# A recurrent mixer begins at step 15 + 7m instead of with pass m, inside a pipelined mixture of experts

## The reference

```python
xn = layernorm(x)
# the mixer, per sequence
xx = shift(xn) - xn
r, alpha, g = sigmoid((xn + xx*x_c) @ W_c.T)      # c = r, a, g
decay = exp(-softplus((xn + xx*x_w) @ W_w.T))
k = tanh((xn + xx*x_k) @ W_k.T);  v = (xn + xx*x_v) @ W_v.T
state_t = state_{t-1} * decay_t + alpha_t * k_t * v_t    # along the 256 tokens
m = r * state;  mn = groupnorm(m, groups of 8 channels) * gn_w + gn_b
s = (mn * g) @ W_out.T + b_out
# the experts, on all 4096 tokens: 4 rounds over the same 4 experts
cur = xn
for rnd in range(4):
    top2 of cur @ Wg[rnd] + bg[rnd]; cw = their softmax weights
    cur = cur + sum_e cw_e * (gelu(cur @ W1[e] + b1[e]) @ W2[e] + b2[e])
out = x + s * silu(cur)
```

## The kernel before

| stage | VectorE, ahead of `g_low_part` | TensorE, behind `down(s)` | ScalarE, ahead of `hidden` |
|---|---|---|---|
| 0 | `mixer_input` job 0 (L620 to L632) | `project` r, w: 6 matmuls | |
| 1 | `mixer_input` job 1 | `project` a, g | `take_rw` |
| 2 | `mixer_input` job 2 | `project` k, v | `take_ag` |
| 3 | `mixer_scan` (L638 to L644) | `turn_mixer`: 2 transposes | `take_kv` |
| 4 | `mixer_norm` (L651 to L660, 17 instructions) | | |
| 5 | | `turn_mixer`: 2 transposes | |
| 6 | `mixer_gate` (L667 to L674) | `W_out`: 3 matmuls (waits for `go_ready`) | |
| 7 | | | `take_s`: writes `s` over `xn_t[:, m]` |

## Time and profile before

### The profile page before, as it was taken

How to read it: one execution, slowest core, us unless ns; L and a number is a source line. 1 busy time by engine, 2 the same in 40 slices (tenths; PEclk the granted TensorE clock), 3 DMA queues, 4 the chain that set the end, 5 groups by cost and what they waited for, 6 DMA issues and landing times.

```text
span 860.7 us, 10675 instructions
## 1 busy us (share of the span) xinstructions
PE 806.1 (94%) x3640; PEld 648.5 (75%) x3640; DVE 748.0 (87%) x1442; ACT 641.4 (75%) x882; POOL 150.4 (17%) x167
## 2 busy tenths in 40 slices
PE   3788999899999999999999999999999999999994
PEld 3566777677778888788878888788878888788883
DVE  7799999999989888887988978897988879898884
ACT  3466767677768887878778887788878888688872
POOL 6022241331111111111111111011111111111111
PEclk7799999999999999999999999999999999999997
DMA  7123442343335342443325332344315433263534
GB/s 218 50 34 90 86 86 39 85 87 95 77 57 134 93 99 37 114 100 70 86 37 148 92 94 38 87 99 98 95 29 146 118 95 60 60 165 95 132 66 85
DMA packets 40581, 76.94 MB, mean 89 GB/s; under 512 B 6480, under 2 KB 18896, under 8 KB 36432
## 3 DMA queue, kind: packets, MB, share of 16 engines
q0 software_dynamic: 18432, 33.56, 23.0%
q1 hardware_dynamic: 21808, 42.69, 15.6%
q10 hardware_dynamic: 288, 0.02, 0.0%
HBM read 40.34 MB, written 2.36 MB: 50 GB/s over the span
## 4 chain that ended last, share of the span: by engine, by line
PE 66%; DVE 25%; ACT 5%; issue 3%; DMA 1%; SPq 0%; DVEq 0%; ACTq 0%; POOLq 0%
PE h_bank L767 10%; PE h_bank L766 10%; PE h_bank L765 10%; PE y_bank L811 10%; PE y_bank L807 10%; PE y_bank L806 10%; DVE g_lo L566 6%; ACT g L377 3%; DVE tmp L577 2%; ACT g_hi L381 2%; PE p_bank L765 2%; PE p_bank L767 1%; PE p_bank L766 1%; DVE xm L624 1%; DVE lgt L526 1%
## 5 line engine op out<-in xcount | busy, mean ns | idle before, releaser
L377 ACT ACTIVATE g<-h_bank,b_c 128x512 f32<-128x512 f32 x512 | 329.8, 681 | 98.7 <-PE h_bank L767 97.5
L566 DVE TENSOR_TENSOR g_lo<-g,g_hi 128x1024 fp32r<-128x1024 f32 x256 | 309.0, 1224 | 72.5 <-ACT g_hi L381 70.9
L381 ACT ACTIVATE g_hi<-g 128x1024 fp32r<-128x1024 f32 x256 | 271.7, 1061 | 8.1
L346 POOL DMA_DIRECT2D cur<-tmp x128 | 114.0, 891 | 693.6 <-DVE tmp L577 558.7
L765 PE MATMUL h_bank<-cur_lo,w_hi 128*128 128x512 f32 x512 | 207.5, 405 | 0.0
L767 PE MATMUL h_bank<-cur_hi,w_hi 128*128 128x512 f32 x512 | 204.8, 400 | 0.0
L766 PE MATMUL h_bank<-cur_hi,w_lo 128*128 128x512 f32 x512 | 204.2, 399 | 0.0
L806 PE MATMUL y_bank<-g_hi,w_hi 128*128 128x512 f32 x512 | 202.5, 396 | 0.0
L807 PE MATMUL y_bank<-g_hi,w_lo 128*128 128x512 f32 x512 | 202.2, 395 | 0.0
L811 PE MATMUL y_bank<-g_lo,w_hi 128*128 128x512 f32 x512 | 141.0, 396 | 0.5 <-DVE g_lo L566 0.4
L767 PEld LDWEIGHTS h_bank<-cur_hi,w_hi 128*128 128x128 f32 x512 | 97.3, 190 | 23.6
(11 more groups left out here) (115 smaller groups left out, 581.2 us busy)
## 6 DMA issues: line engine op xcount, KB each, us to landing
cw_b<-cw_scratch SPq DMA_DIRECT2D x32, 1024.0 KB, 5.7
cur<-tmp POOLq DMA_DIRECT2D x128, 256.0 KB, 3.4
cur<-in_x SPq DMA_DIRECT2D x8, 256.0 KB, 4.8
xr<-in_x SPq DMA_DIRECT2D x8, 256.0 KB, 5.5
out<-o SPq DMA_DIRECT2D x8, 256.0 KB, 3.5
g<-in_w SPq DMA_DIRECT2D x4, 256.0 KB, 5.5
cw_scratch<-cw SPq DMA_DIRECT2D x32, 8.0 KB, 1.4
cw_b<-in_proj_t SPq DMA_DIRECT2D x1, 384.0 KB, 3.3
```

Of the source, the lines that this page charges most:

```text
L346: pool.dma_start(cur[:, s // E % NB * BLK:(s // E % NB + 1) * BLK], tmp[:, t % 2, :], accum_op=ALU.add).then_inc(summed, DMA)
L377: nc.scalar.activation(g[:, gb, ft * BLK:(ft + 1) * BLK], hb[ft][:, :], ACT.Gelu_apprx_tanh, bias=b1_c[:, e * FT + ft:e * FT + ft + 1]).th ...
L381: nc.scalar.activation(g_hi[:, gb, h], g[:, gb, h], ACT.Copy).then_inc(g_hi_done, 1)
L566: nc.vector.tensor_tensor(g_lo[:, gb, h], g[:, gb, h], as_f32(g_hi[:, gb, h]), ALU.subtract).then_inc(g_lo_done, 1)
```

## The change

Sequence m's stage 0 moves from step 8m to step 15 + 7m, and its other stages follow in consecutive steps. The mixers are thus 7 steps apart instead of 8: none in steps 0 to 14, and stage 7 of sequence m falls in the same step as stage 0 of sequence m + 1. The last sequence, 15, begins at step 120 as before. Everything else (layer norm, router, splits, experts, output) keeps its step. Within a step, VectorE now runs the mixer's stage ahead of all other work of that step; before, in steps 3 of the ending passes, `end_output` came ahead of `mixer_scan`. TensorE runs it behind `down` and the logits, ahead of the output's turns. No DMA is moved and SyncE's and GpSimd's queues are untouched.

```diff
+MIX_FROM, MIX_EVERY = 15, 7
...
+        def mixers_at(s):
+            return [(m, s - MIX_FROM - MIX_EVERY * m) for m in range(SEQS) if 0 <= s - MIX_FROM - MIX_EVERY * m < 8]
...
 # ScalarE
-                first = {1: take_rw, 2: take_ag, 3: take_kv, 7: take_s}
...
                 for t in range(8):
-                    if i == PASSES - 1 and t == 7:
-                        take_s()
-                    else:
-                        hidden(8 * i + t + 1, (t + 1) % 4, (t + 1) % 2, first.get(t), between.get(t))
+                    for m, stage in mixers_at(8 * i + t):
+                        if stage in TAKES:
+                            TAKES[stage](m)
+                    if 8 * i + t + 1 < STEPS:
+                        hidden(8 * i + t + 1, (t + 1) % 4, (t + 1) % 2, between.get(t))
...
 # VectorE
                     s = 8 * i + t
+                    for m, stage in mixers_at(s):
+                        if stage == 0:
+                            mixer_input(m, 0, (P_R, P_W))
+                        elif stage == 1:
+                            mixer_input(m, 1, (P_A, P_G))
+                        elif stage == 2:
+                            mixer_input(m, 2, (P_K, P_V))
+                        elif stage == 3:
+                            mixer_scan(m)
+                        elif stage == 4:
+                            mixer_norm(m)
+                        elif stage == 6:
+                            mixer_gate(m)
                     if t == 0:
-                        mixer_input(i, 0, (P_R, P_W))
                         if i == 0:
                             norm_stats(2 * BLK)
...
 # TensorE
             def project(i, job, kinds):
                 pe.wait_ge(xm_ready, 6 * i + 2 * job + 2)
-                if job > 0:
+                if i + job > 0:
                     pe.wait_ge(p_empty, JOBS * i + job)
...
+                    for m, stage in mixers_at(8 * i + t):
+                        if stage == 0:
+                            project(m, 0, (P_R, P_W))
...
+                        elif stage == 6:
+                            pe.wait_ge(go_ready, 2 * m + 2)
+                            pe.wait_ge(p_empty, JOBS * m + J_S)
+                            mm3(pb[:, 0:LEN], wo_hi[:, :], wo_lo[:, :], go_hi[:, :], go_lo[:, :]).then_inc(p_full, 1)
+                    if t == 2 and ending(i):
+                        turn(r_jobs[i, "end_even"], z[:, 0, :], TPB, z_ready, b + 1)
```

More of the change, by code:

```diff
@@ L364, in router_tanh, with hidden @@
                 nc.scalar.activation(lg_th[p, :], lg_d[p, :], ACT.Tanh).then_inc(lgth_ready, 1)
-            def hidden(s1, e, gb, first=None, between=None):
-                if first is not None:
-                    first()
+            def hidden(s1, e, gb, between=None):
                 if s1 == 0:
@@ L383, in hidden @@
                         between()
-            def one_pass(i):
[L386 to L404, removed]
-                first = {1: take_rw, 2: take_ag, 3: take_kv, 7: take_s}
@@ new lines, in take_rw, with take_ag @@
+            def take_rw(m):
+                act.wait_ge(p_full, JOBS * m + J_RW + 1)
+                nc.scalar.activation(rw[:, :, :], pb[:, :].rearrange("p (a t) -> p a t", a=2), ACT.Tanh,
+                                     scale=0.5).then_inc(p_empty, 1)
+            def take_ag(m):
+                act.wait_ge(p_full, JOBS * m + J_AG + 1)
+                nc.scalar.activation(ag[:, :, :], pb[:, :].rearrange("p (a t) -> p a t", a=2), ACT.Tanh,
+                                     scale=0.5).then_inc(p_empty, 1)
@@ new lines, in take_kv, with take_s @@
+            def take_kv(m):
+                act.wait_ge(p_full, JOBS * m + J_KV + 1)
+                nc.scalar.activation(kv[:, 0, :], pb[:, 0:LEN], ACT.Tanh)
+                nc.scalar.activation(kv[:, 1, :], pb[:, LEN:2 * LEN], ACT.Copy).then_inc(p_empty, 1)
+            def take_s(m):
+                act.wait_ge(p_full, JOBS * m + J_S + 1)
+                nc.scalar.activation(xn_t[:, m, 1:LEN + 1], pb[:, 0:LEN],
+                                     ACT.Identity, bias=vec[:, 2:3]).then_inc(p_empty, 1)
@@ L407, in one_pass @@
+            TAKES = {1: take_rw, 2: take_ag, 3: take_kv, 7: take_s}
+            def one_pass(i):
                 between = {}
@@ L705, in one_pass @@
                     elif t == 1:
-                        mixer_input(i, 1, (P_A, P_G))
                         if ending(i):
@@ L709, in one_pass @@
                     elif t == 2:
-                        mixer_input(i, 2, (P_K, P_V))
                         if i == 0:
@@ L717, in one_pass @@
                             end_output(b, r_jobs[i, "end_even"])
-                        mixer_scan(i)
                         if norming(i):
                             store_block(4 * i + 4, i * (2 * BLK) + 2 * BLK, r_jobs[i, "norm_even"])
-                    elif t == 4:
-                        mixer_norm(i)
                     elif t == 5:
@@ L726, in one_pass @@
                     elif t == 6:
-                        mixer_gate(i)
                         if i + 1 < SPLIT_PASSES:
@@ L856, in one_pass @@
                     down(8 * i + t, t % 4, t % 2)
[L857 to L868, removed]
+                    if t == 0 and i <= SPLIT_PASSES:
+                        logits_one(2 * i + 1, r_jobs[i, "logits_odd"])
                     elif t == 4 and norming(i):
@@ L872, in one_pass @@
                         logits_four(2 * i + 2, r_jobs[i, "logits_four"])
[L873 to L880, removed]
+                    for m, stage in mixers_at(8 * i + t):
+                        if stage == 0:
+                            project(m, 0, (P_R, P_W))
+                        elif stage == 1:
+                            project(m, 1, (P_A, P_G))
+                        elif stage == 2:
+                            project(m, 2, (P_K, P_V))
+                        elif stage == 3:
+                            turn_mixer(m, J_MIXED, mixed, m_ready)
+                        elif stage == 5:
+                            turn_mixer(m, J_MN, mn, mn_ready)
+                        elif stage == 6:
[4 more added lines that the diff above has]
+                        turn(r_jobs[i, "end_even"], z[:, 0, :], TPB, z_ready, b + 1)
+                    elif t == 6 and ending(i):
+                        turn(r_jobs[i, "end_odd"], z[:, 1, :], TPB, z_ready, b + 2)
                     elif t == 7 and i == PASSES - 1:
```

## The result

The kernel after the change takes 847.97 us (median of 5 runs, 847.81 to 848.68) against 862.31 us: the ratio is 0.9833, 95% interval 0.982 to 0.9846. The forecast was 848.4 us. The profiled execution took 848.68 us with a span of 846.8, the longest of the five; before it was 862.53, so the two profiles lie 13.85 us apart.

The account below looks back on a forecast made before the run. VectorE was taken to set passes 0 to 2, nearly pass 3, and PE the rest. 862.5 - 17.5 (passes 0 to 3) + 3.4 (passes 4 to 15) = 848.4 us; 846 to 851 at 0.50, range 843.5 to 855.

Parts of the forecast that it names:

- Passes 0 and 1: They lose their mixers and PE takes over from VectorE as bound: 46.6 and 49.5 us, against 59.05 and 56.55.
- Passes 2 and 3: VectorE gets 1.98 us more in each: pass 2 56.1 us; pass 3 52.4, its time without work taking the addition.
- tight-packing rival: VectorE's gaps in passes 2 and 3 are filled wholly, 53.6 + 50.8 us; kernel time 844.3; chance 0.15.
- The sum of the four: Passes 0 to 3 together: 204.6 us against 222.1 before, 17.5 saved.
- Passes 4 to 15: PE sets them: its added mixer work costs + 3.9 us, changed waits behind scores give - 0.5; net + 3.4.
- The waits behind the scores: PE's waits in odd passes 5 to 13, behind the router's scores: 4.5 us in all against 5.0 before.
- The rule for a stage behind scores: After a router's scores VectorE is about 5.1 us behind PE, whatever went before; stage 3 then gives 1.0 wait.
- Collisions: Rival: `g_lo`'s limit is 1 us tighter or lags last longer; 13 sequences cost 0.5 each; 854.9 us; chance 0.17.
- the limit: For `g_lo`: VectorE's lag, all work ahead and 2.3 us must stay within 10.7; stage 4 with a split 9.9.
- The other chains: Rival, early passes: `cw_b` late by 1 us in four turns, GpSimd's tiles twice: + 6, 854.4 us; chance 0.12.
- The clock: Rival, slower than before: PE waits bring 1.2 GHz spells, about 1.6 us each; all nine give 862.8; chance 0.04.
- nine waits of 1 us or more: PE waits expected in the new order: six in steps 15 to 30 and three later.

Follow-up runs that it names:

- run without sequence 0: Kernel before (sequence m at step 8m) with the mixer of sequence 0 left out altogether: 849.62 us, ratio 0.9852.
- spread run: Kernel after with the stages of sequences 0 and 1 spread over chosen steps 5 to 29, away from scores, stage 4 away from stores and splits: 842.57 us, ratio 0.9771.
- run with the old starts: Kernel after with sequence m starting at step 8m again, so only the order inside a step differs from the kernel before: 862.35 us, ratio 1.0.
- stage behind: Kernel after with VectorE running the mixer's stage behind the step's other work instead of ahead of it: 854.09 us, ratio 0.9905.
- run with one more instruction: Kernel after with the instruction that squares `cen` done twice in stage 4, 0.45 us more of VectorE per sequence: 850.81 us.
- evenly spread run: Kernel after with the stages of sequence 0 in every odd step 1 to 15 and of sequence 1 in every odd step 15 to 29: 851.34 us, ratio 0.9876.

## Why the prediction was right

**Passes 0 and 1** (46.6 and 49.5 predicted, 46.80 and 49.65 measured). VectorE set them, and without the mixer PE's load does. The run without sequence 0 shows it apart from everything else: 12.8 us for work that is worth 2.8 in pass 8. The bounds I had given (up to 2 us more for each) weren't needed. In pass 1 PE's own pace, from the last matmul of `down(7)` to that of `down(15)`, is 47.26 us, and VectorE's lag grows by 2.40 in step 15, where 2.43 was taken for stage 0. A turn waited 0.43 us for GpSimd in step 11, where 0.5 was taken.

**Passes 2 and 3** (56.1 and 52.4 predicted, 55.65 and 52.26 measured). VectorE's work rose by 1.41 and 1.74, where 1.98 was said for each. Pass 3's time without VectorE work fell from 3.57 to 1.73 us and took in the added work, as forecast. Pass 2's didn't (2.57 and 2.65), against the tight-packing rival. Why it wasn't filled isn't shown; the spread run shows that the same work, put partly in pass 1, frees time in pass 2. The sum of the four was to save 17.5. It saved 17.76 from 37.00 and 18.4 from the loop's first product, so the sum was 0.9 short.

**Passes 4 to 15** (+ 3.4 predicted, + 3.87 measured). The waits behind the scores were to be 1.0, none, 1.6, 0.8 and 1.1 in steps 46, 62, 78, 94 and 110. They are 0.93, none, 1.55, 0.72 and 0.40. The rule for a stage behind scores held to 0.1 us each time; for `g_lo` in step 110 the list shows less than I said. The terms of the sum were off in two ways. TensorE's work was taken as 13 mixers and stages 3, 5 and 6 of sequence 2, + 3.9. But stage 2 of that sequence falls in step 31, and its `project` comes behind `down(31)`, at 239.42, where it delays pass 4: + 4.6. And the list understates each wait. TensorE's matmuls begin 0.233 us apart but are drawn 0.39 long, so a listed wait begins about 0.16 late. From start to start the five waits of before hold PE up for 5.8 us and those of after for 5.0, small ones of 0.1 to 0.2 included: - 0.8, where - 0.5 was taken. 4.6 - 0.8 is 3.8, against 3.87 measured.

So the sum was 0.9 short in the gain and 0.5 short in the price. That 848.4 lies only 0.4 from the median is in part the luck of two small errors against each other; each part of the mechanism is in the traces.

**Collisions.** This rival had the limit right but not its reach: stage 4 with a split has 0.8 us to spare, so the kernel after pays nothing there, and 1.36 us more would cost it 0.5 each time.

**The other chains.** `cw_b` was in time in passes 0 and 1: VectorE's only idle time ahead of L582 that I find there is 0.2 us, for an accumulation (`cur<-tmp`). The chain through GpSimd cost 0.4 us.

**The clock.** Of the waits in steps 15 to 30, one was followed by a spell, at 128.33 us:

```profile
128.00:132.00 4.00, 3.67 (x12) 3.09 (x13) 3.90 (x7) 1.29 (x2) 0.00 (x0) 0.59 0.91 291
```

The kernel before has two in its loop, not one: besides that of the earlier trace rows there is one behind a wait of 2.05 us at 39.41, which I had overlooked though the earlier trace rows has 0.97 for pass 0:

```profile
39.60:43.00 3.40, 3.40 (x12) 2.92 (x12) 3.23 (x15) 1.29 (x2) 0.00 (x0) 0.50 0.00 0
```

One spell fewer hardly takes part in the difference, because a spell costs little where VectorE sets the pace. The run with the old starts was at the lower clock for 3.4 us more in its first three passes than the kernel before, and its first four passes, from the loop's first product, took 222.5 us against 222.4. The spell of the kernel after cost nothing (above). The prediction's 1.6 us for each is thus an upper end, not a price. I had expected nine waits of 1 us or more; five came.

## What to carry to other kernels

Read busy shares by stage, not over the span: work that must be done somewhere costs the bound engine's price where its engine is the bound (12.8 us here) and only its other engine's share elsewhere (2.8 us), so moving it can save most of its price without removing any work. Before moving, work out for each step how far the engine behind lags and what the other engine wants first; that account, from some 30 rows, gave the waits of the passes that TensorE sets their steps here, and three of four their length to 0.1 us. And it finds a better schedule than an even one: two sequences of sixteen placed by it gave 5.4 us more, the same two spaced evenly lost 3.4.

## What the runs showed of the hardware

The lower clock doesn't follow from a wait's length alone. With waits of 1.97 us (before), 1.92 (after) and 4.23 (stage behind) the granted clock fell to the 1.2 GHz level for 3.4 us, and in the last case for 6.8 (0.50 over 128.97 to 135.80). But the run with one more instruction had the same wait of 1.92 as the kernel after, at 127.71, and its clock stayed at 1.00 (above); the evenly spread run had waits of 2.12 and 2.15 us in steps 1 and 3 and its granted clock over that pass was 1.00:

```profile
37.00:95.80 58.80, 53.35 (x241) 42.19 (x240) 55.31 (x139) 41.56 (x59) 12.21 (x12) 1.00 0.33 72
```

So a kernel with such waits has such spells in one run and not in the next. What one of 3.4 us costs depends on who sets the pace: nothing in steps 14 to 18, 1.5 us in steps 28 to 29. The Trainium skill, "TensorE: Matmul & The Clock Gate", section "HAM oscillation — how this bites in real kernels", ties the lower clock to idle gaps, and to longer ones than the 1.92 us behind which it fell here. The traces agree that every spell inside a loop came with a gap, but they disagree on its length, and not every gap brought one.

GpSimd's layer norm tiles took 2.9 us per pair twice and then 4.65 us in pass 1 after:

```profile
96.69 2.90 POOL L181 TENSOR_SCALAR o<-cur,mean,rstd 128x128 f32<-128x128 f32 x2
...
101.05 4.65 POOL L181 TENSOR_SCALAR o<-cur,mean,rstd 128x128 f32<-128x128 f32 x2
```

VectorE was less loaded than before in that pass (41.87 us against 54.26), so its mean load doesn't set their length. The Trainium skill, "SBUF — State Buffer", section "SBUF: two separate sides", has the two engines exclude each other by instruction; that the third pair ran beside the split and two `g_lo` instructions of VectorE's would fit it, but no run here separated them.
